# Token rows scattered in two halves and kept in one tensor, with the zero fill and the contexts moved

## What is computed

```
def _token_moe(h, gw, gb, w1, b1, w2, b2):
    cw = _combine_weights(h @ gw + gb)      # softmax over the best 2 of 8
    out = jnp.zeros_like(h)
    for e in range(E):
        out = out + _ffn(h, w1[e], b1[e], w2[e], b2[e]) * cw[..., e:e + 1]
    return out
```

## Time and profile before

| | |
|---|---|
| time before, median of 3 runs | 1652.86 us (1650.78 to 1659.54) |
| the profiled execution's own time | 1668.06 us |
| its span, first to last instruction | 1666.6 us |
| TensorE busy (products) | 1549.3 us, 93% |
| VectorE / ScalarE / GpSimd busy | 746.5 / 680.6 / 242.9 us |
| mean granted TensorE clock, of 1.00 | 0.962 |
| moved by DMA | 156.91 MB, mean 94 GB/s |

### The profile page before, as it was taken

One profiled execution on the slowest core, in us unless ns is written; L12 is line 12 of the kernel. 1 busy time (PEld: TensorE's weight loads), 2 busy tenths in 40 slices (PEclk: granted clock), 3 DMA queues, 4 the chain that ended last, 5 costly groups with the idle time before them and its releaser, 6 DMA issues.

```text
span 1666.6 us, 32165 instructions
## 1 busy us (share of the span) xinstructions
PE 1549.3 (93%) x12101; PEld 1280.3 (77%) x12101; DVE 746.5 (45%) x2634; ACT 680.6 (41%) x2151; POOL 242.9 (15%) x381
## 2 busy tenths in 40 slices
PE   7999999789989999998699977999999999999986
PEld 5787887688977777776599966778987777777865
DVE  3535565411126676865011165771124444444466
ACT  2615433222117676654133334543334444344452
POOL 2022210000001121211311142146000000000000
PEclk9999999799999999988799988989999999999999
DMA  9500011359410100400799810327930001000000
GB/s 352 191 1 1 1 42 38 114 180 309 54 48 7 55 2 2 181 2 10 253 324 336 283 44 15 103 91 229 300 127 1 1 1 38 1 2 1 1 1 23
DMA packets 103354, 156.91 MB, mean 94 GB/s; under 512 B 12264, under 2 KB 80992, under 8 KB 102632
## 3 DMA queue, kind: packets, MB, share of 16 engines
q1 hardware_dynamic: 97520, 143.79, 26.3%
q0 software_dynamic: 3648, 9.44, 1.7%
q10 hardware_dynamic: 2048, 1.84, 0.4%
HBM read 147.84 MB, written 11.93 MB: 96 GB/s over the span
## 4 chain that ended last, share of the span: by engine, by line
PE 73%; ACT 7%; DVE 5%; issue 3%; DMA 2%; POOL 2%; another core or an unknown queue 0%; POOLq 0%; ACTq 0%; DVEq 0%
PE psum L581 46%; PE psum L678 6%; PE psum L662 5%; PE psum L702 5%; PE psum L968 5%; ACT arena L889 4%; DMA expert_out<-arena 1%; PE psum L955 1%; POOL token_rows L1272 1%; ACT arena L903 1%; PE psum L710 1%; DVE arena L801 1%; PE psum L537 1%; PE psum L547 1%; PE psum L1683 1%
## 5 line engine op out<-in xcount | busy, mean ns | idle before, releaser
L889 ACT ACTIVATE arena<-arena,rowmin 112x375 f32<-112x375 f32 (+1 forms) x584 | 292.6, 507 | 187.9 <-DVE rowmin L801 187.7
L581 PE MATMUL psum<-arena,region 128*128 128x112 f32 (+2 forms) x1920 | 326.7, 327 | 5.6 <-DMA arena<-in_ctxT 2.5
L581 PEld LDWEIGHTS psum<-arena,region 128*128 128x128 f32 x1920 | 262.8, 197 | 66.9 <-issue 5.7
L581 PE MATMUL psum<-region,arena 128*125 128x128 f32 (+4 forms) x1632 | 231.3, 291 | 9.8 <-DVE arena L790 3.7
L581 PEld LDWEIGHTS psum<-region,arena 128*125 128x125 f32 (+2 forms) x1632 | 196.4, 184 | 44.0 <-issue 18.7
L678 PEld LDWEIGHTS psum<-identity,arena 112*125 112x125 f32 (+1 forms) x1240 | 143.2, 178 | 59.0 <-ACT arena L903 17.2
L678 PE MATMUL psum<-identity,arena 112*125 112x112 f32 (+1 forms) x1240 | 167.5, 280 | 16.5 <-ACT arena L903 5.0
L581 PE MATMUL psum<-arena 128*128 128x128 f32 (+4 forms) x896 | 141.4, 315 | 0.0
L662 PE MATMUL psum<-arena 32*112 32x375 f32 (+3 forms) x912 | 133.7, 477 | 0.5 <-DVE arena L779 0.4
L581 PEld LDWEIGHTS psum<-arena 128*128 128x128 f32 (+2 forms) x896 | 125.7, 191 | 10.6 <-issue 0.3
L949 POOL COPY arena<-rinv 112x128 f32<-112x128 f32 x136 | 34.0, 293 | 591.7 <-DVE rinv L824 569.0
(11 more groups left out here) (304 smaller groups left out, 1905.1 us busy)
## 6 DMA issues: line engine op xcount, KB each, us to landing
stream<-in_moe_w SPq DMA_DIRECT2D x36, 1024.0 KB, 7.3
arena<-in_moe_w SPq DMA_DIRECT2D x36, 1024.0 KB, 7.4
arena<-in_ctxT SPq DMA_DIRECT2D x32, 375.0 KB, 4.2
stream<-in_e_wg SPq DMA_DIRECT2D x8, 512.0 KB, 4.5
stream<-in_e_wu SPq DMA_DIRECT2D x8, 512.0 KB, 5.7
stream<-in_e_wd SPq DMA_DIRECT2D x8, 512.0 KB, 6.6
region<-in_e_wg SPq DMA_DIRECT2D x8, 512.0 KB, 7.4
region<-in_e_wu SPq DMA_DIRECT2D x8, 512.0 KB, 8.3
```

Source lines behind the costliest of these rows:

```text
L581: last = pe.matmul(dst, l, r, start=(i == 0), stop=(i == n - 1))
L889: last = act.activation(e, e, ACT.Exp, bias=rowmin[:, j, n:n + 1], scale=-1.0, accum_out=rowsum[:, j, h:h + 1])
```

## The change

1. `token_rows` holds seven chunks of 128 rows for each expert at a fixed place, and two spare chunks: 58 chunks. A token's row no longer depends on how many chunks the other experts use. `token_outputs` is gone: each chunk's outputs are written over its own rows, and the gathers read them there. Chunks past those in use read the first spare chunk and write the second.
2. The row numbers of the first group are computed and its eight scatters issued before the gates of the second group are done; the second group's follow. The steps of the first lie inside the second group's `second_norm`, between its sums and its application.
3. VectorE writes for each chunk the row to read (`tok_base`) and to write (`tok_put`); GpSimd reads both into registers, three times before it waits for the scatters and twice for each chunk in the loop.
4. One zero fill of `token_rows` stands on SP's queue behind the second group's masks of l2, and the two at the start are gone.
5. The first group's contexts of l2 are loaded right behind the expert rows; block 4 is laid out anew in `arena` so that their places are free.
6. The weights of chunk 1 are loaded right behind those of chunk 0, without waiting for the scatters.

```diff
-        expert_rows = arena[0:T, 0:2 * B * C].rearrange("s (b h f) -> s b h f", b=B, h=2)
-        xnT_all = cut(arena, KC * B * T).rearrange("p (k b t) -> p k b t", k=KC, b=B)
+        n = off["c"] + 2 * S2
+        expert_rows = arena[0:T, n:n + 2 * B * C].rearrange("s (b h f) -> s b h f", b=B, h=2)
...
-        tok_rows = nc.dram_tensor("token_rows", ((MAX_TURNS * TOK_SLOTS + 4) * P, C), F32, kind="Internal").ap()
-        tok_outs = nc.dram_tensor("token_outputs", (MAX_TURNS * TOK_SLOTS * P, C), F32, kind="Internal").ap()
+        tok_rows = nc.dram_tensor("token_rows", ((SPARE + 2) * P, C), F32, kind="Internal").ap()
...
+            def clear_rows():
+                load(tok_rows.rearrange("(c p) f -> c p f", p=P), A["zeros"].unsqueeze(0).broadcast_to([SPARE + 2, P, C]),
+                     s_zero)
...
             for i in range(E1 // EX_SLOTS):
                 rows_of_turn(i)
+            for j in range(LANES):
+                context("l2", 0, j)
...
             for it in range(ITERS):
                 for j in range(LANES):
-                    context("l2", it, j, p_l2x["v_out"].at(0, a2.tiles - 1, j) if it else None)
                     if it:
+                        context("l2", it, j, p_l2x["v_out"].at(0, a2.tiles - 1, j))
                         sp.wait_ge(*p_l2x["rowmin_ready"].at(0, a2.tiles * a2.steps - 1, j))
                     load(maskb[j].bitcast(I32), A["mask2"][it * LANES + j], s_maskl[j])
+                if it:
+                    clear_rows()
...
             chunk_expert(0, 0)
+            chunk_expert(0, 1)
             sp.wait_ge(s_scat, 16 * PAIRS)
-            for r in range(1, TOK_SLOTS):
+            for r in range(2, TOK_SLOTS):
...
-            g.wait_ge(s_zero, 32)
-            g.wait_ge(s_route, 8)
-            g.wait_ge(*p["normed"].at(0, f_norms(0)[NORM_B2], LANES - 1))
-            for b in range(B):
-                for k in range(TOP2):
-                    n = b * TOP2 + k
-                    g.indirect_dma_start(tok_rows, bass.IndirectOffsetOnAxis(ap=tok_slot[:, n:n + 1], axis=0),
-                                         hrow[b % LANES][:, b // LANES, :], None).then_inc(s_scat, 16)
-            g.wait_ge(s_scat, 16 * PAIRS)
-            g.wait_ge(s_tid, 2)
+            g.wait_ge(s_zero, 16)
+            for i in range(ITERS):
+                g.wait_ge(s_route, 5 if i == 0 else 9)
+                g.wait_ge(*p["normed"].at(0, f_norms(0)[NORM_A2 + i], LANES - 1))
+                for j in range(LANES):
+                    for k in range(TOP2):
+                        n = (i * LANES + j) * TOP2 + k
+                        g.indirect_dma_start(tok_rows, bass.IndirectOffsetOnAxis(ap=tok_slot[:, n:n + 1], axis=0),
+                                             hrow[j][:, i, :], None).then_inc(s_scat, 16)
+            g.wait_ge(s_tid, 4)
...
+            begin = [rows_at(0, r) for r in range(2)]
+            g.wait_ge(s_scat, 16 * PAIRS)
             for r in range(2):
-                chunk_rows(0, r)
+                chunk_rows(begin[r], r)
...
+            def slots_of(i, to):
+
+                of = slice(i * P // 2, (i + 1) * P // 2)
+                held_by = slice(0, (i + 1) * P // 2)
+                pe.matmul(to[0:T, 0:P // 2], before, picked[:, of], start=True, stop=False)
+                pe.matmul(to[0:T, 0:P // 2], count[held_by, :], groups_before[held_by, of], start=False, stop=False)
+                pe.matmul(to[0:T, 0:P // 2], whole_of.broadcast_to([E2, T]), chunks_before[:, of], start=False,
+                          stop=True).then_inc(s_rmm, 1)
...
+                    if l == 0 and it:
+                        pe.wait_ge(s_picks, TOP2)
+                        pe.matmul(bank[4][0:P // 2, 0:T], picked[:, 0:P // 2], one_col[0:T, 0:1].broadcast_to([T, T]),
+                                  start=True, stop=True).then_inc(s_rmm, 1)
+                        pe.wait_ge(s_rconst, 16 * 7)
+                        pe.wait_ge(s_route, 2)
+                        slots_of(0, bank[5])
...
                 norm_stats(v, p, 0, n, summed_out, lambda j: p["proj_out"].at(it, 0, j))
+                if l == 0 and it:
+                    slots_of(0, bank[5], 2, 2)
                 norm_apply(v, p, 0, n, summed_out, dst)
```

More of the change, by code:

```diff
@@ L331, in flamingo @@
         idf = arena[0:1, 3 * LB + 2400:3 * LB + 2430]
+        tok_put = arena[0:1, LB + off["w"] + 1024:LB + off["w"] + 1024 + MAX_TURNS * TOK_SLOTS].bitcast(I32)
+        past_use = arena[0:1, LB + off["w"] + 1050:LB + off["w"] + 1050 + MAX_TURNS * TOK_SLOTS]
+        whole_of = arena[0:E2, 3 * LB + 2062:3 * LB + 2063]
+        chunks_left = arena[0:1, 3 * LB + 2064:3 * LB + 2064 + E2]
+        basef = arena[0:1, 3 * LB + 2432:3 * LB + 2462]
+        SPARE = E2 * MAX_OF
         tok_hid = [arena[:, s * LB + 2048:s * LB + 2048 + 8 * P] for s in range(2)]
@@ L982, in flamingo @@
         at["n"] = 0
+        xnT_all = cut(arena, KC * B * T).rearrange("p (k b t) -> p k b t", k=KC, b=B)
+        hbuf = [arena[:, at["n"] + h * 4 * T:at["n"] + (h + 1) * 4 * T] for h in range(2)]
+        assert at["n"] + 8 * T <= off["c"]
         xn_all = cut(arena, B * C)[0:T, :].rearrange("t (b c) -> t b c", b=B)
@@ L1472, in _ @@
                     attend_scalar(act, af[l], p, it, own=(1,) if it else ((1, 2, 4, 5), (4, 5, 6))[l])
+                    if l == 0 and it:
+                        act.wait_ge(s_rmm, 1)
+                        act.copy(count[0:P // 2, :], bank[4][0:P // 2, 0:T]).then_inc(s_route, 1)
                     if l == 0:
@@ L1854, in _ @@
                           stop=True).then_inc(s_rmm, 1)
-                pe.wait_ge(s_route, 1)
-                pe.wait_ge(s_rconst, 16 * 7)
+                pe.wait_ge(s_route, 6)
+                slots_of(1, bank[2])
                 pe.matmul(bank[1][0:E2, 0:T], of_expert, count, start=True, stop=True).then_inc(s_rmm, 1)
-                pe.wait_ge(s_route, 3)
-                pe.matmul(bank[2][0:T, 0:P], before, picked, start=True, stop=False)
-                pe.matmul(bank[2][0:T, 0:P], count, groups_before, start=False, stop=False)
-                pe.matmul(bank[2][0:T, 0:P], used.broadcast_to([E2, T]), chunks_before, start=False,
-                          stop=True).then_inc(s_rmm, 1)
-                pe.matmul(bank[3][0:T, 0:E2], used.broadcast_to([E2, T]), chunks_upto, start=True,
+                pe.wait_ge(s_route, 11)
+                pe.matmul(bank[3][0:T, 0:E2], used.broadcast_to([E2, T]), chunks_upto, start=True, stop=True)
+                pe.matmul(bank[3][0:T, E2:2 * E2], used.broadcast_to([E2, T]), ident[0:E2, 0:E2], start=True,
                           stop=True).then_inc(s_rmm, 1)
@@ L2309, in summed_out, with slots_of @@
                 return bank_s[j][0:T, 0:C]
+            def slots_of(i, src, products, done):
+                of, half = slice(i * SEQ_ITEMS, (i + 1) * SEQ_ITEMS), P // 2
+                v.wait_ge(s_rmm, products)
+                v.tensor_tensor(place[:, of, :], src[0:T, 0:half].rearrange("t (g e) -> t g e", e=E2), picks[:, of, :],
+                                ALU.mult).then_inc(s_route, 1)
+                v.wait_ge(s_route, done + 1)
+                v.tensor_reduce(placef[:, of], place[:, of, :], AX_X, ALU.add).then_inc(s_route, 1)
+                v.wait_ge(s_route, done + 2)
+                v.tensor_copy(tok_slot[:, of], placef[:, of]).then_inc(s_route, 1)
             def second_norm(p, l, it, dst):
@@ L2376, in _ @@
                     continue
[L2378 removed]
+                slots_of(1, bank[2], 4, 6)
+                v.wait_ge(s_rmm, 5)
                 v.tensor_scalar(fill, whole, bank[1][0:E2, 0:1], None, ALU.is_lt).then_inc(s_route, 1)
[L2380 removed]
+                v.wait_ge(s_route, 10)
                 v.tensor_reduce(used, fill, AX_X, ALU.add).then_inc(s_route, 1)
[L2382 removed]
+                v.wait_ge(s_rmm, 6)
                 n = MAX_TURNS * TOK_SLOTS
```

73 lines of the change are left out of this document (44 added, 29 removed).

## The result

The changed kernel took **1644.73 us**, the median of 9 runs (from 1636.12 us), beside 1652.86 for the kernel before: a ratio of **0.993**, 95% interval 0.991 to 0.995. In one of its runs, 2390.6 us, the granted clock was 0.591; it is left out of the ratio, and the median of the other eight is 1643.59. Run again later with its experiments, the same kernel took 1641.28, ratio **0.9908** (0.9882 to 0.9934). The forecast was 1641, between 1635 and 1649, a ratio of 0.9929.

What follows compares the result with a forecast made beforehand. The prediction took TensorE to bound the kernel, so only gaps where it stands could be regained: 2.5 us at the contexts plus 9.2 to the first product, 11.7 off 1652.86, gives 1641 us, range 1635 to 1649.

Steps and rivals of the forecast that it cites:

- The sum: Whole kernel: 2.5 us from the l2 contexts plus 9.2 from routing to first product, 11.7 in all.
- the way to the first product: From routing to the first chunk's first hidden product: a gain of 9.2 us, from 7.4 to 10.5.
- Contexts: Start of l2: loading the first contexts earlier removes TensorE's wait, gaining 2.5 us, from 0 to 2.7.
- The slip of the second norm: Second group's second norm: the added slot work delays turning, gate products and gates by 2.6 us, 2.0 to 3.3.
- I take 1.6: Second group's second norm: the three slot products after the count take 1.6 us, against 1.9 at twice the width.
- The scatters: GpSimd's queue: eight issued from 778.4, eight from 788.9, the last ending at 798.8 us, not 808.06.
- rival (d): Both scatter halves run consecutively at the old place, or masks take the contexts' gain: 1649 to 1653 us; chance 0.08.
- Rival (b): Scatters don't run beside VectorE; held until its address chain ends at 794, giving 1656 us; chance 0.05.
- The estimate of 20 us: First eight scatters: waiting for descriptors beside VectorE's shared-port use would cost 20 us more and lose; the forecast took 0.
- From the last scatter to the product: Before the chunk loop: scatters land by 800.4 to 803.4, reads take 5.1 us, first hidden product at 809.5.
- The fill: SP's queue after l2's masks: on two engines the 58-chunk fill ends at 742.6, weights in at 763; cost 0.
- What costs nothing: Removed start fill, GpSimd's register loads per chunk (1.6 us), VectorE's chunk addresses and changed output-store addresses: all free.

Runs made afterwards that it cites:

- before again: The kernel before the change, unedited, run and profiled a second time: 1653.24 us, ratio 0.9992.
- Experiments 4: The changed kernel with all sixteen scatters waiting for the second group's slots: 1648.98 us, ratio 0.9968 against the kernel before.
- 7: The changed kernel with the weights of chunk 1 loaded only after the scatters have landed: 1640.89 us, ratio 0.9913 against the kernel before.
- 8: The changed kernel with the weights of chunks 2 and 3 held until the first chunk's rows are turned: 1641.48 us, ratio 0.9908 against the kernel before.
- the three edits together: The changed kernel with a 64-chunk fill, chunk 1's weights behind the scatters and those of chunks 2 and 3 held until rows are turned: 1638.7 us, ratio 0.9895.

## Why the prediction was right, and where not

The sum was 11.7 us; the change measured 8.1 in one comparison (1652.86 to 1644.73) and 14.3 in another (1655.53 to 1641.28). By stretches it is 4.0 to 5.5 for the contexts, 8.1 from the projection to the first product (48.5 against 40.4), and 0.5 to 0.8 lost on the first products of the loop: 11.4 to 12.9. The two causes were the right ones. That the sum fits so well is in part luck, since its errors cancel: the contexts were put 1.5 to 3 us too low, the way to the first product 1.1 too high, and the loss in the loop was not in it.

- **Contexts, 2.5 with a range of 0 to 2.7.** Right in mechanism, too small: 4.0 to 5.5. The step that failed is "TensorE starts at about 493.2 and not 495.73", taken as the whole price of the wait. It left out the products behind it, which run at a granted clock of 0.50 at first, after TensorE has stood. The masks were not late, as said.
- **The slip of the second norm, 2.6.** Measured from the start of the output projection (770.47 in the trace of before, 766.35 after) the applications end 1.3 us later and the counts start 1.5 later. "I take 1.6" for the three products was the mis-sized term: at 64 columns they overlap to 1.04 (770.74 to 771.78). Moreover, part of the slip lies where VectorE had waited for rstd (0.33 in the earlier trace rows).
- **The scatters.** Two times eight, but in one chain, so rival (d) has fallen too: the second slots stand at 15.96 us after the projection's start instead of 17.4. The last issue ends 27.0 after it; 28.3 was forecast, 37.6 it was. No scatter was stretched: 937, 942 and 1206 ns are the numbers of the kernel before (937/942/1205), with VectorE busy for 4.9 of the 9.9 us of the first eight. Rival (b) has fallen. The estimate of 20 us from the Trainium skill, SBUF — State Buffer, section A bandwidth-pool intuition that's wrong, is not borne out by any run here; its figure is for a copy, and VectorE's work beside these eight is the end of the norm and small operations of the gates.
- **From the last scatter to the product.** 1.64 to 4.6 was the range for the landing, and the sum went "nearer to the early end". This is the second term that failed: the last scatter landed in 4.5, and the reads in 6.5, not "5.1 as before" (before again: 6.4). From the end of the last issue to the product it took 13.3 us where 10.7 was forecast and 10.6 to 11.5 it was: 2.6 more than the sum had, of which the shorter chain makes good 1.3. Experiments 4, 7 and 8 show why: the experts' weights move beside them. The register loads were hidden behind the landing.
- **The fill.** "22.6 GB/s each" was low: 55 GB/s on two engines. The queue moved on at 714, where the fill alone was to last until 742.6, and the constants went out 38 us before TensorE wanted them, not 12. The 0 was right.
- **What costs nothing.** The start: from the span's begin to SP's load for l2 the kernels with the old fills take 488.8 to 492.2 us and those without 487.3 to 493.6. They differ by 6 us among themselves, as much as the two comparisons do. GpSimd's extra loads in the loop: 60.2 us of waiting for outputs are left of 62.9 in the earlier trace rows, and behind the first 64 products the loop takes 141.8 us in both kernels, so they cost nothing. The 0.5 to 0.8 us are those products at a lower clock.

Two comparisons of one kernel gave 8.1 and 14.3 us, 6 apart, so no term of this sum could be judged by a total; the stretches of the traces could.

## What to carry to other kernels

Read what stands behind a wait of TensorE as well as the wait: here 2.6 us of waiting cost 4 to 5.5, and 3.1 us cost 5.4, because the products after it ran at a lower clock; warm-up products that last until the data land give that part back even when the data come no sooner. Look at the outermost dimension of every large DMA before its size, and at what is queued behind it. When a step is moved beside transfers that it was free of before, price its landing by the loaded row.

## What the runs showed that I had not expected

- One broadcast fill of 8.0 MB with 61 rows ran at 32 GB/s and held SP's queue until 865.6, with stalls of up to 44.6 us for single loads; 7.6 MB with 58 ran at 55 GB/s; 8.4 MB with 64 raised the core's traffic to 318 GB/s.
- With two engines SP's queue did not stop at the first load behind the fill (667.05), but at the seventh (674.87).
- What a short stand of TensorE does to the clock isn't one thing. It fell to 0.50 around the end of stands of 2.54 and 2.59 us (before), 3.11 (the change), 2.39 (all scatters late) and 2.00 and 1.25 (the three edits together). It stayed at 1.00 through stands of 1.27 (warm-up in the context wait) and of 1.51 and 0.42 (18 warm-ups). It was back at 1.00 at 498.55 in the first execution of before, 2.8 us behind the first product, and at 498.17 in the second, 5.8 us behind it, after nearly equal stands. What decides it stays open; no run varied it by itself.
- *To scatter* was 106.1 in three executions and 107.5 in two with an identical program up to that point. The whole difference lies ahead of the projection (98.9 to 99.0 us from `raw_g` against 100.4), at clocks of 0.83 and 0.75 in the same 10 us. Why the clock falls there in the one and the other way was not tried.
